# A four-layer attention and FFN kernel: another order for the head of both attentions, and GpSimd and VectorE exchange work

## What is computed

```python
x = x + tanh(g_xattn[0]) * attention0(layernorm(x), ctx, ctx, mask)     # (8, 100, 512), ctx (8, 722, 512), 16 heads
x = x + tanh(g_ffn[0])   * ternary_ffn(layernorm(x))                    # 512 -> 2048 -> 2048 -> 2048 -> 512
x = x + tanh(g_xattn[1]) * (attention1(layernorm(x), ctx, ctx) @ Wo.T + bo)
x = x + tanh(g_ffn[1])   * bitlinear_ffn(layernorm(x))
# each attention: q = x Wq + bq, k = ctx Wk + bk, v = ctx Wv + bv, softmax(q k / sqrt(32)) v
```

## Time and profile before

| | us |
|---|---|
| median of 3 runs | 1663.46 |
| lowest and highest | 1661.58, 1665.76 |
| the profiled execution, its own time | 1663.37 |
| its span in the profile | 1661.6 |
| TensorE busy in the span | 1592.4 (96%) |
| VectorE, ScalarE, GpSimd busy | 1043.0, 973.8, 375.0 |

### The profile page before, as it was taken

How to read it: one execution, slowest core, us unless ns; L and a number is a source line. 1 busy time by engine, 2 the same in 40 slices (tenths; PEclk the granted TensorE clock), 3 DMA queues, 4 the chain that set the end, 5 groups by cost and what they waited for, 6 DMA issues and landing times.

```text
span 1661.6 us, 25627 instructions
## 1 busy us (share of the span) xinstructions
PE 1592.4 (96%) x9298; PEld 1445.2 (87%) x9298; DVE 1043.0 (63%) x1864; ACT 973.8 (59%) x2014; POOL 375.0 (23%) x492
## 2 busy tenths in 40 slices
PE   5899999999988999999999999979999999999898
PEld 5788999899977999999999997768899989998655
DVE  6367877788786453223644435546777777778786
ACT  4367776767665455444544444236667666766565
POOL 2022121212133222222322222002111111113641
PEclk9999999999998999999999999999999999999999
DMA  6666776776582225554366535356666666657400
GB/s 194 136 159 178 189 177 169 186 192 176 135 202 66 93 96 168 178 188 160 111 215 218 201 127 170 106 114 155 174 185 167 160 177 185 167 141 190 158 12 28
DMA packets 146232, 257.74 MB, mean 155 GB/s; under 512 B 40916, under 2 KB 90196, under 8 KB 145968
## 3 DMA queue, kind: packets, MB, share of 16 engines
q1 hardware_dynamic: 145648, 255.79, 54.6%
q10 hardware_dynamic: 448, 0.14, 0.0%
HBM read 187.46 MB, written 58.57 MB: 148 GB/s over the span
## 4 chain that ended last, share of the span: by engine, by line
PE 88%; DVE 5%; ACT 3%; issue 1%; DMA 1%; POOL 1%; SPq 0%; ACTq 0%; DVEq 0%; POOLq 0%
PE ps L999 32%; PE ps L688 16%; PE ps L684 14%; PE ps L735 8%; PE ps L747 7%; PE ps L722 2%; PE ps L725 2%; PE ps L805 2%; PE ps L940 2%; PE ps L953 1%; ACT P L1662 1%; PE ps L724 1%; PE ps L723 1%; DVE nmax L1162 1%; DMA P<-in_x 1%
## 5 line engine op out<-in xcount | busy, mean ns | idle before, releaser
L999 PE MATMUL ps<-ah_f,wh_f 128*128 128x400 f32 (+1 forms) x1296 | 447.3, 346 | 0.8 <-issue 0.8
L999 PE MATMUL ps<-al_f,wh_f 128*128 128x400 f32 (+1 forms) x1296 | 445.8, 344 | 0.0
L1993 POOL TENSOR_TENSOR cxl<-raw,cxh 128x384 fp32r<-128x384 f32 (+1 forms) x120 | 118.9, 1012 | 656.7 <-ACT cxh L1627 650.0
L1552 DVE TENSOR_TENSOR wl_f<-raw_f,wh_f 128x1024 fp32r<-128x1024 f32 x85 | 103.9, 1224 | 238.0 <-POOL wh_f L2175 238.0
L999 PEld LDWEIGHTS ps<-ah_f,wh_f 128*128 128x128 f32 x1296 | 246.4, 190 | 2.4 <-issue 1.5
L999 PEld LDWEIGHTS ps<-al_f,wh_f 128*128 128x128 f32 x1296 | 246.6, 190 | 0.0
L1162 DVE TENSOR_REDUCE nmax<-ps 100x1 f32<-100x722 f32 x256 | 220.7, 904 | 38.1 <-PE ps L724 34.5
L1662 ACT ACTIVATE P<-ps,nmax 100x722 f32<-100x722 f32 x256 | 219.8, 861 | 31.8 <-DVE nmax L1162 31.6
L1671 ACT ACTIVATE PT<-ps 128x400 fp32r<-128x400 f32 x384 | 166.9, 505 | 81.7 <-PE ps L735 80.5
L1168 DVE TENSOR_TENSOR PT<-ps,PT 128x400 fp32r<-128x400 f32 x384 | 196.8, 568 | 3.5
L1927 ACT ACTIVATE raw_f<-wl_f 128x1024 f32<-128x1024 f32 x88 | 93.5, 1062 | 178.4 <-DVE wl_f L1552 178.3
(11 more groups left out here) (191 smaller groups left out, 2574.7 us busy)
## 6 DMA issues: line engine op xcount, KB each, us to landing
KS<-kd SPq DMA_DIRECT2D x192, 361.0 KB
raw_f<-in_h SPq DMA_DIRECT2D x64, 512.0 KB, 4.4
raw_f<-in_gud SPq DMA_DIRECT2D x48, 512.0 KB, 4.4
raw<-in_ctx SPq DMA_DIRECT2D x64, 192.0 KB, 3.6
kd<-ksh SPq DMA_DIRECT2D x64, 192.0 KB, 2.2
kd<-ksl SPq DMA_DIRECT2D x64, 192.0 KB, 2.4
raw_f<-in_w SPq DMA_DIRECT2D x24, 512.0 KB, 3.5
raw<-in_ctx SPq DMA_DIRECT2D x64, 169.0 KB, 4.3
```

The costliest lines, as they stand in the source:

```text
L999: return e.matmul(o, p, q, start=start, stop=stop)
L1552: e.tensor_tensor(wl[:, z, :], raw[:, r, :], raw32(wh[:, z, :]), ALU.subtract).then_inc(v_ul, 1)
L1993: e.tensor_tensor(m.cx[1][:, k, off:off + n], m.raw[:, k, off:off + n], raw32(m.cx[0][:, k, off:off + n]), ALU.subtract).then_inc(g_cx, 1)
```

## The change

Both heads get the same order on TensorE: all seven K jobs, then turns and V jobs in turn, the first queries, more turns and V jobs, three groups of the second queries, `scores(0)`, the fourth group, V4. `scores(0)` waits only for the queries' first bank (`a_q` 5) and `turn` for all of them. The exponentials stand ahead of the fourth group and of V4 on ScalarE.

VectorE forms all low halves of the first batch's context. GpSimd no longer does; it makes the mask (attention 0), the low parts of two query weights (`BY_POOL`), the inverse roots (`input_roots`: the `roots` that the kernel had, ten instructions, on four columns), and in attention 1 the add of the residual (`add_residual`), while VectorE does the multiplication only (`scaled_out`). ScalarE loses `root`, does the tanh later and no longer waits for the constants first. x gets eight buffers instead of four.

The core of the diff (of the orders of TensorE and VectorE only what is new; the removed ones stand in the functions above; a line of "..." leaves lines out):

```diff
+ADDED = (0, 1, 2, 3, 5, 7, 4, 6)
+BY_POOL = (6, 7)
...
         def wait_ctx(w, L, b, half, k):
-            if (b, half) == (0, 1):
-                w.wait_ge(v_cx, 4 * L + k + 1)
+            if b == 0:
+                w.wait_ge(v_cx, 8 * L + 4 * half + k + 1)
             else:
-                w.wait_ge(g_cx, 60 * L + 8 * b + 4 * half + k + 1 - (4 if b else 0))
+                w.wait_ge(g_cx, 56 * L + 8 * (b - 1) + 4 * half + k + 1)
+
+        def wait_low_w(w, L, i):
+
+            if i in BY_POOL:
+                w.wait_ge(g_wl, 2 * L + BY_POOL.index(i) + 1)
...
                 if L == 0:
                     for b in range(4):
                         load_x(m, b)
-                    for i in range(4, 10):
+                    for i in range(4, 8):
                         load_w(L, m, i)
+                    for b in range(4, 8):
+                        load_x(m, b)
+                    load_w(L, m, 8)
+                    load_w(L, m, 9)
+                    store_k(L, m, *K00[1:])
                     for c in range(2):
-                        w.wait_ge(v_mask, c + 1)
+                        w.wait_ge(g_mask, c + 1)
                         e.dma_start(mrow[:, c, :], raw32(m.KS[0:B, 0, c, :])).then_inc(d_mrow, 16)
-                    store_k(L, m, *K00[1:])
                     store_k(L, m, *K01[1:])
                     load_w(L, m, 10)
                     load_w(L, m, 11)
                     store_k(L, m, *K10[1:])
-                    load_x(m, 4)
-                    load_x(m, 5)
+                    for k in range(4):
+                        load_ctx(L, m, 1, 0, k)
                     store_k(L, m, *K11[1:])
-                    load_x(m, 6)
-                    load_x(m, 7)
                     w.wait_ge(d_mrow, 32)
                     load_k(L, m, 0, 0)
                     store_k(L, m, *K20[1:])
-                    for k in range(4):
-                        load_ctx(L, m, 1, 0, k)
-                    spread_q(L, m, 0)
                     store_k(L, m, *K21[1:])
                     store_k(L, m, *K30[1:])
                     load_k(L, m, 0, 1)
+                    spread_q(L, m, 0)
                 else:
                     for i in range(4, 12):
                         load_w(L, m, i)
-                    for n in range(3):
-                        store_x(n)
                     store_k(L, m, *K00[1:])
+                    store_x(0)
+                    store_k(L, m, *K01[1:])
+                    store_x(1)
+                    store_k(L, m, *K10[1:])
+                    store_x(2)
+                    store_k(L, m, *K11[1:])
                     store_x(3)
-                    store_k(L, m, *K01[1:])
+                    store_k(L, m, *K20[1:])
                     store_x(4)
-                    store_k(L, m, *K10[1:])
+                    store_k(L, m, *K21[1:])
                     store_x(5)
-                    for j in (K11, K20, K21, K30):
-                        store_k(L, m, *j[1:])
+                    store_k(L, m, *K30[1:])
                     for n in (6, 7):
                         store_x(n)
...
                     if i:
                         w.wait_ge(a_exp, LAST * L + 2 * i)
+                    else:
+                        w.wait_ge(a_q, 8 * L + 5)
...
                 def turn(i):
                     w.wait_ge(a_exp, LAST * L + 2 * i + 2)
+                    w.wait_ge(a_q, 8 * L + 8)
...
+                if L:
                     w.wait_ge(v_res, 1)
...
+                job(K00)
+                if L:
                     w.wait_ge(v_res, 2)
...
+                for j in (K01, K10, K11, K20, K21, K30):
+                    job(j)
+                turn_x(0)
+                turn_x(1)
+                job(V0)
+                turn_x(2)
+                turn_x(3)
+                job(V1)
+                query(0)
+                turn_x(4)
+                turn_x(5)
+                job(V2)
+                turn_x(6)
+                turn_x(7)
+                job(V3)
+                query(1, range(3))
+                scores(0)
+                query(1, [3])
+                job(V4)
...
+                def scaled_out(n):
 
                     b = RESIDUALS[n]
...
+                    e.tensor_tensor(tmp[0:S, b, :], ps[0:S, b, :], s3, ALU.mult).then_inc(v_res, 1)
 
                 def stats_x(b):
                     if L == 0:
...
+                        w.wait_ge(d_xl[b], 16)
                     else:
...
+                        w.wait_ge(g_res, ADDED.index(b) + 1)
+                    me.then(e.bn_stats(st[0:S, b, :], xf[b] if L else m.xtile[b]))
+                    me.settle()
+                    e.bn_aggr(mv[0:S, b, :], st[0:S, b, :]).then_inc(v_sx, 1)
 
                 def normal_x(b):
...
+                    w.wait_ge(g_rt, 2 * L + b // 4 + 1)
+                    e.tensor_scalar(m.xtile[b], xf[b] if L else m.xtile[b], mv[0:S, b, 0:1], rq[0:S, 1, b:b + 1],
+                                    ALU.subtract, ALU.mult).then_inc(v_xn, 1)
 
                 if L:
                     e.tensor_copy(idb[:, :], ident[:, :]).then_inc(v_id, 1)
+                for k in range(4):
+                    split_w(k)
+                    low_ctx(0, k)
+                for k in range(4):
+                    low_ctx(1, k)
                 if L == 0:
...
+                    w.wait_ge(d_const, 48)
+                    for l in range(2):
+                        i = 4 * COL[f"bq{l}"]
+                        e.tensor_scalar(cols[:, i:i + 4], cols[:, i:i + 4], SCALE, None, ALU.mult).then_inc(v_bq, 1)
+                    low_job(K00)
+                    low_job(K01)
+                    stats_x(0)
+                    stats_x(1)
+                    low_job(K10)
+                    stats_x(2)
+                    stats_x(3)
+                    split_w(4)
+                    split_w(5)
+                    low_job(K11)
+                    low_job(K20)
+                    split_w(8)
+                    split_w(9)
+                    low_job(K21)
                     for b in range(4):
                         normal_x(b)
+                    low_job(K30)
+                    split_w(10)
+                    split_w(11)
+                else:
+                    for i in (4, 5, 8, 9, 10, 11):
+                        split_w(i)
+                    w.wait_ge(d_s3, 16)
+                    w.wait_ge(a_g, 1)
+                    me.then(e.tensor_scalar(s3, s3, G["f0"][0:S], None, ALU.mult))
+                    me.settle()
+                    w.wait_ge(p_u, UNITS)
+                    for n in range(5):
+                        scaled_out(n)
                     low_job(K00)
+                    scaled_out(5)
+                    scaled_out(6)
                     low_job(K01)
...
+                    scaled_out(7)
+                    stats_x(0)
+                    stats_x(1)
                     low_job(K10)
...
+                    stats_x(2)
+                    stats_x(3)
                     low_job(K11)
...
                     low_job(K20)
...
+                    for b in range(4):
                         normal_x(b)
                     low_job(K21)
                     low_job(K30)
...
+                turned_x(0)
+                turned_x(1)
+                low_job(V0)
+                turned_x(2)
+                turned_x(3)
+                low_job(V1)
+                for b in range(4, 8):
+                    stats_x(b)
+                for b in range(4, 8):
+                    normal_x(b)
+                turned_x(4)
+                turned_x(5)
+                low_job(V2)
+                turned_x(6)
+                turned_x(7)
+                low_job(V3)
                 peak(0)
                 peak(1)
+                low_job(V4)
...
+                def low_wq(i):
+                    w.wait_ge(a_wh, 12 * L + i + 1)
+                    e.tensor_tensor(m.wq[1][:, i % 4, :], m.stage[i % 6], raw32(m.wq[0][:, i % 4, :]),
+                                    ALU.subtract).then_inc(g_wl, 1)
+                def add_residual(n):
+                    b = ADDED[n]
+                    w.wait_ge(v_res, RESIDUALS.index(b) + 1)
+                    w.wait_ge(d_xl[b], 32)
+                    e.tensor_tensor(xf[b], xf[b], tmp[0:S, b, :], ALU.add).then_inc(g_res, 1)
+                def input_roots(half):
+                    w.wait_ge(v_sx, 8 * L + 4 * half + 4)
+                    roots(S, 4 * half, 4 * half + 4, g_rt)
...
+                if L == 0:
+                    w.wait_ge(d_mask, 16)
+                    me.then(e.tensor_copy(mf, m32))
+                    me.settle()
+                    me.then(e.tensor_scalar(mf, mf, -1.0, 10000.0, ALU.add, ALU.mult))
+                    me.settle()
+                    e.tensor_copy(m.KS[0:B, 0, 0, :], mf).then_inc(g_mask, 1)
+                    w.wait_ge(g_mask, 1)
```

(76 more changed lines are left out.)

271 lines of the change are left out of this document (42 added, 229 removed).

## The result

The changed kernel takes 1654.67 us (median of 11 runs, 1650.54 to 1657.18), the kernel before 1663.46 (11 runs, 1659.44 to 1669.44). The ratio is 0.9945, with a 95% interval of 0.9929 to 0.9961: 9 us faster, where 18 were forecast and 10.5 was the least that the range allowed. The profiled execution of after took 1650.54 us, span 1648.7. It is the lowest of the 11: the stretch between the two heads, whose instructions are the same, took 963.6 us in it and 969.1 in the profile of before. So I read each head by itself. Attention 0's runs from the start to the end of V5, attention 1's from the FFN's last matmul to the end of V5.

What follows compares the result with a forecast made beforehand. TensorE was taken as busy nine tenths nearly everywhere, its larger gaps at the heads of both attentions. Gains of 14.2 us in attention 1 and 3.8 in attention 0, 18.0 together, took 1663.37 to 1645 us, range 1638 to 1653.

Steps and rivals of the forecast that it cites:

- step (2): Attention 0: K00's store, issued near 15 us behind 5.9 MB of loads at 310 to 335 GB/s, lands near 22.
- K10's store: Attention 0: issued at 26.5 us behind 0.5 MB of weights, it takes 3.6 us and lands at 30.1.
- K20's store: Attention 0: issued at 32 us behind three KS loads, it lands at 41.0 (38.5 to 43).
- V0 goes on: Attention 0: V0, half done since 38 us, waits for work behind K30's parts and resumes at 42.9.
- rival B: Attention 0: K10's store takes 10.1 us, not 3.6; 6.5 us more, 1651.5, up to 1653; chance 0.12.
- The waits taken away: Attention 1: TensorE's waits for K banks, residual, normalized x, queries and exponentials go, together 11.6 us.
- the clock: Attention 1: V matmuls, turns and scores no longer run at the lower clock after long waits, 4.0 us gained.
- V0's wait: Attention 1: the first turns' normalizations stand ahead of K21's low part on VectorE, costing 1.1 us.
- Rival C: Both heads: GpSimd slows beside VectorE, roots at twice 3.6 us; 3.6 and 0.8 us lost each, 1654; chance 0.05.
- Rivals A: Attention 0: K20's store lands sooner, in 4 us, so V0 goes on 4.9 us earlier; 1640; chance 0.22.
- D: Both heads: GpSimd's root chain so slow, 15 us instead of 3.6, that the kernel gets slower; 1668 or more; chance 0.03.
- E: Attention 1: `scores(0)` waits for `QS`, landings 6 us instead of 3.1, K21's chain 2 us more; 1650; chance 0.10.

Runs made afterwards that it cites:

- k00_first: Changed kernel with K00's store in attention 0 ahead of the loads of x 4 to 7 and V weights 8 and 9; 1648.84 us, one run.
- x_late: Changed kernel with only the loads of x 4 to 7 moved behind K00's store in attention 0; 1650.15 us, one run.
- k20_first: Changed kernel with the stores of K20, K21 and K30 in attention 0 ahead of batch 1's context and the KS loads; 1647.59 us, one run.
- the repair: Changed kernel's attention 1 with x 4 to 7's residual adds after normalizations 0 to 3, their stores behind K30; alone 1654.36 us, one run.
- k10_first: Changed kernel with K10's store in attention 0 ahead of V weights 10 and 11; 1655.82 us, one run.
- stores_first: Changed kernel with the repair, attention 0's K stores ahead of movable loads, x 4 to 7 behind first KS loads; 1650.79 us, 0.9911 of the kernel before.
- two_rows: Second pair of K staging rows in attention 0, against a kernel with reordered K stores and the repair (1639.77 us); 1646.04 us.

## Why the prediction was wrong

**Attention 0: step (2) failed, the others held to within 1 us.** Step (2) is the landing of K00's store. Step by step, forecast and measured: K00's store issued 15 and 16.5 to 17.3; landed 22 and 27.9; K10's store 3.6 and 4.4 us; K20's store issued 32 and 38.6, landing 8.9 and 8.0 us; V0 goes on at 42.9 and 48.95; from the first queries to the end of V5 32.7 and 32.8 us. So K00's landing was 5.9 us late, and the whole chain with it, to 88.5 instead of 82.0. The step added up the bytes ahead of the store, 5.9 MB, and divided them by one rate for all 16 DMA engines, 310 to 335 GB/s "when always fed" (the slices of before give 307 and 314, no more). The engines were not fed alike. The 1.6 MB of x lie on ten engines, 164 KB each, and the rest, 4.2 MB, on all 16, 265 KB each: 429 KB on each of the ten and 265 on each of the six. The six were through by 20.0 us, ahead of the forecast's 22, and the store waited for the ten until 27.9. From 20 us on the rate that the step relied on was not there: 245 GB/s from 20 to 25 us, at a share of 0.73. The change had put four more loads of x ahead of this store. `k00_first` showed that the loads ahead are the cause of the late landing, `x_late` that x has the larger part in it, and `k20_first` that K20's store was late by the loads ahead of it as well. The store was also issued 1.5 to 2.3 us later than forecast. How the 5.9 us divide between the issue and the uneven load no run shows, nor whether x spread over all 16 engines would do as well as x moved behind; that was not run. This is rival B's mechanism, one store further up; B had put its 6.5 us at K10's. That the sum came near B's is luck: K10's store took 4.4 us, not 10.1.

**Attention 1: two terms mis-sized.** The waits taken away were right: of the 12.4 us in the earlier trace rows 11.6 were to go, and 11.1 went (with the first turn's 0.6 counted as new). So was the clock: the turn takes 1.03 us and V jobs behind `scores(1)` 2.8. V0's wait was set at 1.1 and measured 2.7 in all seven profiles without the repair, since the normalizations were priced without GpSimd beside them, and the first turn waited 0.6, which the forecast had at nothing. These 1.6 and 0.6 us and the 0.5 that did not go are the 2.7 by which the head missed 57.6. And I gave V0's wait no clock, which the profiled execution did not need. But in five of the seven profiles the granted clock averaged 0.82 to 0.90 over the 15 us around it (TensorE stood at 1.2 GHz for a part of them), and the head took 61.8 to 63.1 us instead of 60.3. In attention 1, the forecast's rule that a wait costs more than its length was applied to what was removed and not to what was added.

**Rival C was near the truth and mispriced.** GpSimd's roots took 3.6 to 4.3 us in the changed kernel, near the forecast's 3.6 (in `k10_first` and `stores_first` one took 5.1). I had read the rule on shared interfaces as a danger to GpSimd's adds and roots; VectorE was the one held up. By the Trainium skill, SBUF — State Buffer, section Who interferes with whom, VectorE (in its two-port modes, or with two inputs from SBUF) and GpSimd take one pair of ports in turn, and the one that starts second stands still until the other's instruction ends. The trace agrees in the main: 5.71 / 4 = 1.43 us for a normalization is one add of 5.51 / 4 = 1.38 each, and each normalization ended 0.28 us behind its add. But the pair took less than the 1.26 and 0.48 us that the two take alone, 1.74 together, so they still overlap in part, and the adds got longer by a tenth as well. Rivals A, D and E did not come: K20's store took 8.0 us, no root of this kernel took longer than 4.3 us, and `scores(0)` waited in neither head.

**What holds for the whole.** In the profiled execution 6.5 us of attention 0, 2.7 of attention 1 and 1.5 behind it are 10.7, and the stretch between the heads, with the same instructions, gave 5.5 back: 1650.5 instead of 1645.4. That execution alone would have fallen into the range, by this stretch and not by the mechanism. The median is 9.7 above the forecast and 1.7 above the range. The range's upper end stood for a chain of late stores (rival B), and not for such a chain and a late V0 of attention 1 together.

## What to carry to other kernels

Before moving work from between the links of a chain of stores, give each store its place in the queue ahead of every load that could be behind it, and check by when those loads are wanted: here that was worth 14 us of attention 0, and one load put too late made TensorE wait 9 us. When you price the landing of a store in a full queue, count the bytes by DMA engine: here a load of 100 rows went over ten of the 16, and the store waited for these ten. Add up the clock with the waits: the waits of attention 0 were as long as before, and it lost 2.7 us. And price a GpSimd instruction by what VectorE does beside it from SBUF: a normalization of 0.48 us became 1.43.

## What was not expected of the hardware

- A load of x, 100 rows, lands in ten counts of its semaphore and a DMA of 128 rows in 16. Behind eight such loads a store of 128 rows had twelve of its 32 counts by 20.0 us and the last at 27.9.
- VectorE's normalization (SBUF to SBUF, 100x512) takes 0.48 us alone and 1.43 beside a GpSimd add. In `two_rows` a low part of a V weight took 1.88 us beside GpSimd's low part of a query weight (1.28), and the next, behind it, 0.68. In the first us of the changed kernel a low part of context took 2.05 beside the mask's last instruction (2.02), where the next took 0.55; TensorE's first matmul, at 8.92 us, waited for it. Work that reads PSUM kept its time, and so did a `bn_stats` that reads SBUF (0.68 us beside an add, 0.66 to 0.69 alone).
- With the same attention 1, the clock fell at a wait of 2.7 us in five of seven profiles and not in the other two. Between 350 and 450 us behind the head the level differs in the opposite sense, so that 3 to 6 us of difference in the head vanished by the end.
